# Attention, Sinkhorn and output stages on one Trainium2 core: a new order of work within the step

## The reference

```python
x = x + tanh(g_xattn) * xattn(layernorm(x), ctx)   # windows of 128 columns, 8 heads of 32
x = x + tanh(g_ffn) * ffn(layernorm(x))            # 4 streams of 512
```

## Time and profile before

| | us |
|---|---|
| median of 3 runs | 1862.13 |
| lowest and highest | 1848.97 to 1864.48 |
| the profiled execution | 1858.43 |
| its span, first to last instruction | 1856.3 |
| busy: TensorE, VectorE, ScalarE, GpSimd | 1407.3, 1336.4, 1138.3, 822.1 |
| mean granted TensorE clock | 0.879 |

### The profile page before, as it was taken

The page is one execution under the profiler, slowest core; times in us unless marked ns, Lnnn a source line. Parts: engine busy times, 40 slices in busy tenths (PEclk is TensorE's granted clock), DMA queues, the critical chain, the costliest instruction groups (busy, mean ns, idle before and its releaser), DMA issues.

```text
span 1856.3 us, 35823 instructions
## 1 busy us (share of the span) xinstructions
PE 1407.3 (76%) x12448; PEld 864.0 (47%) x12448; DVE 1336.4 (72%) x3566; ACT 1138.3 (61%) x2273; POOL 822.1 (44%) x1373
## 2 busy tenths in 40 slices
PE   2778899898888898888988798888898886522223
PEld 0455556555555455555555455545555554211011
DVE  3343334566678878987888787888787788779987
ACT  3466777877677768776777767766767665411111
POOL 3223334454655573556454655556454634430000
PEclk9799999999999899998999898989999897655656
DMA  8456676665666666665666566665565454421122
GB/s 260 129 153 169 189 201 181 165 169 159 173 187 195 187 181 200 191 181 174 188 181 192 158 174 197 195 189 161 171 172 153 137 127 110 116 79 57 57 93 112
DMA packets 173923, 299.88 MB, mean 162 GB/s; under 512 B 23568, under 2 KB 74640, under 8 KB 169648
## 3 DMA queue, kind: packets, MB, share of 16 engines
q1 hardware_dynamic: 156336, 264.03, 45.2%
q0 software_dynamic: 17408, 33.56, 10.5%
HBM read 179.81 MB, written 67.11 MB: 133 GB/s over the span
## 4 chain that ended last, share of the span: by engine, by line
DVE 28%; PE 19%; POOL 18%; issue 13%; ACT 13%; DMA 5%; SPq 4%; ACTq 0%; POOLq 0%; DVEq 0%
POOL kp L556 9%; PE pr L651 7%; DVE ssum L1209 5%; DMA xc<-in_dram 4%; DVE sa L1210 3%; ACT squares L918 3%; DVE negm L1087 3%; DVE xpre L1226 3%; POOL ctx_hl L484 3%; SPq L412 3%; POOL x_hl L479 2%; DVE otile_odd L1238 2%; PE pr L678 2%; DVE otile_even L1254 2%; DVE sv L1210 2%
## 5 line engine op out<-in xcount | busy, mean ns | idle before, releaser
L1209 DVE TENSOR_REDUCE ssum<-kp 128x16 f32<-128x64 f32 x768 | 182.2, 237 | 154.1 <-POOL kp L556 149.3
L556 POOL TENSOR_TENSOR kp<-ke,sa 128x64 f32<-128x64 f32 x343 | 151.4, 441 | 273.5 <-DVE sa L1210 273.5
L556 POOL TENSOR_TENSOR kp<-ke,sv 128x64 f32<-128x64 f32 x329 | 151.5, 460 | 220.9 <-DVE sv L1210 219.5
L878 ACT ACTIVATE probs<-st_ps,key_bias 128x512 f32<-128x512 f32 x256 | 174.6, 682 | 110.8 <-PE st_ps L752 110.4
L738 PE MATMUL s_ps<-k_st,q_st 97*128 97x128 bf16 x1024 | 104.5, 227 | 145.8 <-DVE negm L1087 128.6
L479 POOL TENSOR_TENSOR x_hl<-xc,x_hl 128x512 bf16<-128x512 f32 x128 | 150.4, 1175 | 138.9 <-ACT x_hl L846 138.8
L651 PE MATMUL pr<-x_hl,wq 128*128 128x512 bf16 x768 | 183.0, 390 | 38.1 <-POOL x_hl L479 38.1
L1087 DVE TENSOR_REDUCE negm<-s_ps 128x4 bf16<-128x512 f32 x256 | 166.5, 650 | 58.1 <-PE s_ps L738 57.6
L651 PE MATMUL pr<-x_hl,wk 128*128 128x512 bf16 x768 | 196.8, 411 | 0.0
L678 PE MATMUL pr<-o_sb,wo 128*128 128x512 bf16 x768 | 188.6, 390 | 0.0
L665 PE MATMUL pr<-wv,ctx_hl 128*128 128x256 bf16 x1536 | 179.9, 274 | 3.5 <-DVE wv L1275 3.5
(11 more groups left out here) (149 smaller groups left out, 3062.9 us busy)
## 6 DMA issues: line engine op xcount, KB each, us to landing
xs<-in_dram SPq DMA_DIRECT2D x128, 256.0 KB, 6.5
xc<-in_dram SPq DMA_DIRECT2D x32, 1024.0 KB, 5.6
ctx_raw<-in_dram SPq DMA_DIRECT2D x32, 1024.0 KB, 7.9
x1c<-in_dram POOLq DMA_DIRECT2D x64, 512.0 KB, 8.4
x_dram<-x1c SPq DMA_DIRECT2D x32, 1024.0 KB, 4.3
q_st<-q_hl SPq DMA_DIRECT2D x384, 64.0 KB
k_st<-k_hl SPq DMA_DIRECT2D x384, 64.0 KB
x1t_even<-x_dram SPq DMA_DIRECT2D x16, 1024.0 KB, 4.9
```

Source lines behind the costliest of these rows:

```text
L556: nc.gpsimd.tensor_tensor(kp[:], ke[:], v, ALU.mult).then_inc(kp_made, 1)
L878: nc.scalar.activation(probs[:, k % 2, :], st_ps[:], ACT.Exp, bias=key_bias[:, b, w:w + 1], scale=SCALE).then_inc(exp_done, 1)
L1209: cf.link(nc.vector.tensor_reduce(s_t, k, AX.X, ALU.add))
```

## The change

TensorE: `values(g - 2)` goes from behind the first banked product to right behind `scores_t(g - 1)`. In `banked_at` the projections and o come ahead of t, lg and pre; sel stays first. ScalarE: `inverse_den` goes ahead of `first_products`, `first_out` and the reads of banked products, and `answer` ahead of those reads. GpSimd: `scale_at` part 1 follows part 0 directly (but for the coefficients); the first ctx split, the first low half of Gelu and both `add_x` stand between parts 1 and 2, as do `variance`, `xstat` and `stat_b`; the second ctx split of r = 2 goes between parts 2 and 3. VectorE: `divide` takes unit g - 2 in place of g - 3 and stands behind half iteration 2 and the second output part; the softmax stages and `return_scales` go from the end of the step to ahead of the first output part.

```diff
@@ banked_at @@
     made = [("sel", f, 0) for f in ffn_at(g, UPC + SELECT_AT)]
-    made += [("t", H, j) for H, j in at_step(g, 2, T_AT)]
-    made += [("lg", H, 0) for H, j in at_step(g, 2, [LOGITS_AT])]
-    made += [("pre", f, t) for f, t in tiles_at(g, "pre")]
     if 0 <= G + 1 < NG:
         made += {0: [("q", G + 1, 0)], 1: [("q", G + 1, 1)], 2: [("k", G + 1, 0)], 3: [("k", G + 1, 1)],
                  4: [("v", G + 1, 0)], 7: [("v", G + 1, 1)]}.get(r, [])
     if 0 <= G - 1 < NG and r in (5, 6):
         made += [("o", G - 1, 2 * (r - 5)), ("o", G - 1, 2 * (r - 5) + 1)]
+    made += [("t", H, j) for H, j in at_step(g, 2, T_AT)]
+    made += [("lg", H, 0) for H, j in at_step(g, 2, [LOGITS_AT])]
+    made += [("pre", f, t) for f, t in tiles_at(g, "pre")]
@@ GpSimd @@
                 for ready in ffn_at(g, COEF_AT):
                     coefficients(ready)
+                scale_at(f, its, 1)
+
+                low = at_step(g, -1, LOW_CTX_AT)
+                for H, t in low[:1]:
+                    split_ctx(H, t)
+                if 0 <= G - 1 < NG and r == 4:
+                    low_gelu(G - 1, 0)
+                if 0 <= G - 1 < NG and r == 7:
+                    add_x(G - 1, 0)
+                if 0 <= G - 2 < NG and r == 0:
+                    add_x(G - 2, 1)
                 if g >= 0 and u == 15 and b + 1 < B:
                     variance(b + 1)
...
                 for part in range(3):
                     for ready in ffn_at(g, STAT_AT + 1 + part):
                         stat_b(ready, part)
-                scale_at(f, its, 1)
-                for H, t in at_step(g, -1, LOW_CTX_AT):
+                scale_at(f, its, 2)
+                for H, t in low[1:]:
                     split_ctx(H, t)
-                if 0 <= G - 1 < NG and r == 4:
-                    low_gelu(G - 1, 0)
-                scale_at(f, its, 2)
                 if 0 <= G - 1 < NG and r == 4:
                     low_gelu(G - 1, 1)
                 for H, t in at_step(g, -2, LOW_X_AT):
                     split_x(H, t)
                 scale_at(f, its, 3)
-                if 0 <= G - 1 < NG and r == 7:
-                    add_x(G - 1, 0)
-                if 0 <= G - 2 < NG and r == 0:
-                    add_x(G - 2, 1)
@@ TensorE @@
                 if 0 <= g - 1 < NU:
                     scores_t(g - 1)
+                if 0 <= g - 2 < NU:
+                    values(g - 2)
                 made = banked_at(g)
...
-                    if n == 0:
-                        if 0 <= g + 1 < NU:
-                            scores(g + 1)
-                        if 0 <= g - 2 < NU:
-                            values(g - 2)
-                if not made:
-                    if 0 <= g + 1 < NU:
+                    if n == 0 and 0 <= g + 1 < NU:
                         scores(g + 1)
-                    if 0 <= g - 2 < NU:
-                        values(g - 2)
+                if not made and 0 <= g + 1 < NU:
+                    scores(g + 1)
@@ ScalarE @@
                     hi_x(H, t)
+                if 0 <= g - 2 < NU:
+                    inverse_den(g - 2)
                 for done, t in tiles_at(g, "first"):
                     first_products(done, t)
                 for pair in range(2):
                     for done, t in tiles_at(g, f"out_{pair}"):
                         first_out(done, t, pair)
+                for n in range(5):
+                    for ready in ffn_at(g, SOFTMAX_AT + n):
+                        answer(ready, n)
+                for n in range(2):
+                    for ready in ffn_at(g, RETURN_AT + n):
+                        answer(ready, 5 + n)
                 made = banked_at(g)
...
-                    if n == 0 and 0 <= g - 2 < NU:
-                        inverse_den(g - 2)
-                if not made and 0 <= g - 2 < NU:
-                    inverse_den(g - 2)
...
-                for n in range(5):
-                    for ready in ffn_at(g, SOFTMAX_AT + n):
-                        answer(ready, n)
-                for n in range(2):
-                    for ready in ffn_at(g, RETURN_AT + n):
-                        answer(ready, 5 + n)
@@ VectorE @@
                 half_at(f, its, 0)
-                if 0 <= g - 3 < NU:
-                    divide(g - 3)
...
                 half_at(f, its, 1)
+                for ready in ffn_at(g, SOFTMAX_AT):
+                    logits(ready)
+                for n, part in enumerate((softmax_first, softmax_last, columns_first, columns_sum, columns_last)):
+                    for ready in ffn_at(g, SOFTMAX_AT + n):
+                        part(ready)
+                for ready in ffn_at(g, RETURN_AT + 1):
+                    return_scales(ready)
                 output_parts(g, 0)
                 half_at(f, its, 2)
                 output_parts(g, 1)
+                if 0 <= g - 2 < NU:
+                    divide(g - 2)
...
                 half_at(f, its, 3)
-                for ready in ffn_at(g, SOFTMAX_AT):
-                    logits(ready)
-                for n, part in enumerate((softmax_first, softmax_last, columns_first, columns_sum, columns_last)):
-                    for ready in ffn_at(g, SOFTMAX_AT + n):
-                        part(ready)
-                for ready in ffn_at(g, RETURN_AT + 1):
-                    return_scales(ready)
```

## The result

The changed kernel takes 1847.91 us (median of 5 runs, 1840.60 to 1850.99) against 1862.13 before; the ratio is 0.993, with a 95% interval of 0.9905 to 0.9955. The forecast was 1808, 2.9% less. The time lies in the stated range, and nearest to the third rival (the gaps only move, 1856). The forecast of the size was wrong. So a difference of a few us between two traces is not told from noise.

What follows compares the result with a forecast made beforehand. VectorE sets the pace in the loop, through its work and gaps; the terms sum to -9.5 us a batch, over 5.3 batches -50, from 1858.4 to 1808 us. The range was 1765 to 1876.

Steps and rivals of the forecast that it cites:

- the third rival: In the loop, the division waits 3.47 us in each chunk, leaving nearly nothing of the gain: 1856 us, chance 0.16.
- splits, add_x, statistics and the division's cover together: VectorE's gaps before half iterations, per batch: splits -2.1, add_x -1.3, statistics -2.7, division's cover +1.1 and -1.0 us.
- the low halves: VectorE's k_hl gaps at r = 4 go because the K projection comes ahead of the transposes: -5.5 us a batch.
- behind the return step: VectorE's wait for the exponential behind the return step goes, once a batch: -3.3 us.
- +1.2 a chunk, +4.8 a batch: VectorE's division waits where ScalarE runs late, by count at r = 4 (0.3 us) and r = 5 (0.9 us).
- "-2.5" for the softmax chunk: VectorE's 3.47 us wait before a division shrinks, the denominator no longer behind outputs and logits: -2.5 us a batch.
- The term of TensorE's late scores: TensorE's scores come late in the loop, 0.5 us a chunk: +2.0 us a batch, bounds 0 and 4.4 a chunk.
- a sign against it: ScalarE idle in answer for longer than 3 us with probs behind it would show the forecast wrong.
- Before step 55 no half iteration runs: Ahead of step 55, TensorE with ScalarE bound the loop and projection order changes nothing: 0, within 5 us either way.
- No cost on the path: The V projection takes k1's bank and waits until some 2.2 us into VectorE's step 4, yet ends before scores are needed.
- The second: Rival: TensorE idles at r = 1 to 3 behind a late division, its clock falls: +32 us, 1890, chance 0.14.
- The first rival: ScalarE keeps ahead, the division never waits, TensorE's slack holds: -16.3 us a batch, 1772 us, chance 0.17.

Runs made afterwards that it cites:

- Experiment 1: The changed kernel with inverse_den directly behind exp_scores on ScalarE, ahead of hi_gelu, hi_ctx, norm_x and hi_x: 1801.46 us, ratio 0.9705.
- experiment 3: The kernel before with only values at the head of TensorE's step, the denominator early, and division of unit g - 2 behind half iteration 2: 1858.41 us, 1.0023.
- experiment 11: The changed kernel with the denominator put back behind ScalarE's first read of a banked product, division left in the step of the values: 1913.35 us, 1.0303.
- experiment 9: The changed kernel with the denominator directly behind the exponential and the first transpose of r = 3 ahead of the K product: 1798.01 us, 0.9676.
- experiment 2: The changed kernel with values, denominator and division (unit g - 3) put back to their old places, all else changed: 1844.60 us, 0.9944.
- experiment 6: The kernel before with only the order of the banked products changed: 1867.46 us, 1.0058.
- experiment 8: The changed kernel with values, denominator and division in their old places, and the first transpose of r = 3 ahead of the K product: 1824.90 us, 0.9829.

## Why the prediction was wrong

**Right: what bounds the loop, and the sum of its gaps.** VectorE's maximum did not become late in the loop (42.8 us of waits, all but 2 in the first 55 steps), its busy time did not fall, and the loop shrank by gaps alone. These are steps 86 to 254 before, then after:

```profile
513.01:1559.67 1046.66, 901.45 (x8124) 554.85 (x8123) 850.98 (x2253) 733.63 (x1472) 565.98 (x940) 0.92 0.62 176
```

```profile
535.95:1543.65 1007.70, 860.56 (x8107) 530.58 (x8105) 862.72 (x2252) 728.31 (x1466) 561.74 (x939) 0.97 0.63 182
```

VectorE's idle time there fell from 195.7 to 145.0 us, by 50.7, and the forecast was 50. That the sum fits so well is in part luck, since its terms missed both ways, as the next paragraphs tell.

**Right: the gaps that close.** In steps 128 to 159 VectorE's idle time in front of half iterations fell from 20.7 to 15.9 us (forecast -6.0 for splits, add_x, statistics and the division's cover together), that of the low halves from 7.1 to 1.0 (forecast -5.5), and that behind the return step from 3.5 to 0.6 (forecast -3.3). The earlier trace rows call themselves the four longest waits of that batch; two others, the 1.81 us for k_hl and one of 1.65 for q_hl, are longer than the 1.52 there. The second was in no term.

**Wrong in size: VectorE's work.** The prediction let it stand. It grew by 11.7 us in steps 86 to 254, which is about what the loop stayed behind its forecast (-39.0 instead of -50), and from 163.9 to 167.1 in steps 128 to 159. Rows of that batch, first before and then after:

```profile
L1238 DVE SCALAR_TENSOR_TENSOR otile_even<-x1t_even,cmat,otile_even 128x512 f32<-128x512 f32 x24 | 21.6, 905 | 0.0
L1238 DVE SCALAR_TENSOR_TENSOR otile_odd<-x1t_odd,cmat,otile_odd 128x512 f32<-128x512 f32 x24 | 21.6, 918 | 0.0
...
L1095 DVE TENSOR_TENSOR o_sb<-av_ps,rden 128x128 f32<-128x128 f32 x32 | 7.7, 242 | 3.8 <-ACT rden L887 3.8
...
L1152 DVE SCALAR_TENSOR_TENSOR logit<-logit,rb,base_sb 128x32 f32<-128x32 f32 x4 | 0.9, 280 | 0.0
```

```profile
L1236 DVE SCALAR_TENSOR_TENSOR otile_even<-x1t_even,cmat,otile_even 128x512 f32<-128x512 f32 x24 | 24.5, 1023 | 0.0
...
L1236 DVE SCALAR_TENSOR_TENSOR otile_odd<-x1t_odd,cmat,otile_odd 128x512 f32<-128x512 f32 x24 | 21.2, 903 | 0.1
...
L1093 DVE TENSOR_TENSOR o_sb<-av_ps,rden 128x128 f32<-128x128 f32 x32 | 9.2, 288 | 9.4 <-ACT rden L887 8.7
...
L1150 DVE SCALAR_TENSOR_TENSOR logit<-logit,rb,base_sb 128x32 f32<-128x32 f32 x4 | 3.0, 811 | 0.0
```

The division takes 288 ns behind an output instruction, 242 where it stood before (+1.5 us). The 48 outputs grew from 43.2 to 45.7, and the four logit instructions, moved to another place, from 0.9 to 3.0; others became shorter. An output that runs beside one of GpSimd's splits takes 1.20 us (median), one with nothing on GpSimd beside it 0.75, so GpSimd's order has a price on VectorE. But 22 of the 48 stand beside a split in both kernels, so more such pairs are not the cause; what made the outputs longer is open. The Trainium skill's page "SBUF — State Buffer", section "Who interferes with whom", has the pair blocking each other; the 1.20 against 0.75 agrees with it. The prediction used it for the multiply and left out the other side.

**Wrong in size: the division's wait.** "+1.2 a chunk, +4.8 a batch" against "-2.5" for the softmax chunk made +2.3; measured was 3.8 to 9.4 us, +5.6 in this batch, and 21.7 to 44.5 in steps 86 to 254. The mechanism was right, and so were its steps r = 4 and 5; r = 3, which it did not name, has 10.1 of the 44.5. The term of TensorE's late scores, +2.0, did not come (2.0 us in all of the loop). In answer ScalarE waits 4.4 us for softmax_first in four of the batches, over the 3 us that the prediction named as a sign against it; what that costs VectorE was not taken apart. Together this batch gave -5.7 instead of -9.5, and the loop's mean is -7.4 a batch.

**The step that failed: "Before step 55 no half iteration runs and TensorE with ScalarE bound the loop; there the projections take the same time in any order: 0, within 5 either way."** These steps took 10.9 us more, and steps 55 to 85, for which the prediction has no term at all, 12.4 more. The forecast of the span was -50 and it came to -17.8: of the 32.2 between them, 23.3 are these two stretches, 11.0 the loop, and -2.1 what lies ahead and behind.

That the projections take the same time is beside the point. VectorE is busy 41% of steps 0 to 54 (111.4 of 268.6 us before), so little covers a division that waits; the rows of step 33 show ScalarE, VectorE and TensorE waiting one for the other. The change put ScalarE's late denominator into that chain, by taking away the step between denominator and division. Experiment 1 shows it: without the lateness steps 0 to 54 take 255.3 us instead of 279.5, steps 55 to 85 164.6 instead of 181.5, both less than before the change, and steps 86 to 254 1005.2 instead of 1007.7. The other traces bear it out. Steps 0 to 54 take 279.5 to 297.7 us in the three kernels that divide in the step of the values with the denominator late (the changed one, experiments 3 and 11), and 255.3 to 269.8 in all eleven others. So the late denominator took 42.3 us of the span, 41.0 of them ahead of step 86. Why steps 55 to 85 lose only when all parts are together is open: they take 181.5 and 182.6 us in the changed kernel and experiment 11, and 160.7 to 170.0 in all others, those of the three places alone (experiment 3, 166.6) among them. The wait for the load of x is not the whole of it: ScalarE's waits for it add up to 15.4 us in the first 64 steps, and 18.9 before the change.

**The bank of the V product.** "No cost on the path" held for the changed kernel (TensorE waits 15.0 us for k_hl in it and 19.8 in experiment 1, and experiment 9, which takes this away, shows no sure gain). By experiments 2, 6 and 8 it held only because the values stand first. Without them it costs 1.2 points (experiments 2 and 8), and alone the new order of products is a loss (experiment 6).

**The rivals.** The second did not come: TensorE does wait long for the division, but its granted clock rose from 0.92 to 0.96 in steps 64 to 254. The third came nearest in time (1856), but partly by luck: it named the right wait, and had it eat up the gain in the loop, where 39.0 us of the gain came, while the loss lies ahead of step 86. The first rival's 1772 has not been reached by any version.

**The parts by themselves**, in points of the time: GpSimd's order -1.15, the three places +0.23, the banked order +0.58, the exchanges -0.29. Their sum, -0.63, is close to the whole change's -0.70. With the denominator directly behind the exponential the three places are -0.63, the sum would be -1.5, and the whole (experiment 1) is -2.95: there the parts help each other. That it is the early values which let the new order of products pay is likely by experiments 2, 6 and 8, but no run has these two alone with the early denominator.

## What to carry to other kernels

When a consumer is moved into the same step as its producer, look at what is queued ahead of the producer on every engine between them, a wait for a DMA included, and move the short instructions that others wait for ahead of the long ones that nobody waits for. Work out each phase of a kernel by itself, the transitions too: the steps ahead of the steady loop, where its busiest engine has time to spare, are not neutral to a reordering; here they lost 23 us while the loop gained 39. When work is moved to another place, price the instructions again as well as the gaps. And when products rotate through banks, an order is also an assignment of banks: list for each product whose read it now waits for.

## What the runs showed of the hardware that was not expected

TensorE's clock did not follow the sum of its waits. In steps 64 to 254 its granted clock is 0.96 after the change, with 139.3 us of waits for the division before the values, and 0.92 before it, with 127.0 us for the maximum in front of the scores and 17.7 in front of the values. But the 139.3 us are 103 waits, 1.35 us in the mean and 3.4 at most, and the 127.0 are 62, 2.05 in the mean and 4.1 at most: fewer and longer waits went with the lower clock. That the length is the cause is not shown.

VectorE's 128 x 128 division, one operand in PSUM, has a median of 228 ns before the change and 291 after it. What goes before it tells the two apart within each kernel (all figures are medians). Before the change 160 of the 256 follow a reciprocal without a wait and take 228 ns, and the 62 that come after a wait behind the maximum take 291. After it, 15 still follow a reciprocal without a wait, 228, and 9 follow the same reciprocal after a wait, 292; those behind an output instruction take 291 to 292.
